# Decay factors of a gated linear attention: one difference for four heads on VectorE and one exponential on ScalarE, in place of four exponentials with a bias

## What is computed

```python
def step(S, inputs):
    qb, kb, vb, lb = inputs
    o_inter = einsum('bhid,bhde->bhie', qb * exp(lb)[..., None], S)
    A = einsum('bhid,bhjd->bhij', qb, kb)
    diff = where(mask, lb[..., :, None] - lb[..., None, :], -inf)
    A = A * exp(diff)
    o_intra = einsum('bhij,bhjd->bhid', A, vb)
    tot = lb[..., -1]
    kd = kb * exp(tot[..., None, None] - lb[..., None])
    S_new = exp(tot)[..., None, None] * S + einsum('bhjd,bhje->bhde', kd, vb)
    return (S_new, o_inter + o_intra)
```

## Time and profile before

| | |
|---|---|
| Median of three runs | 999.23 us (998.97 to 1001.07) |
| Profiled execution | 1001.8 us, its span 1000.1 us |
| TensorE busy | 849.0 us, 85% of the span |
| VectorE busy | 591.0 us, 59% |
| ScalarE busy | 489.6 us, 49% |
| GpSimd busy | 360.4 us, 36% |
| Mean granted TensorE clock | 0.921 of full speed |

### The profile page before, as it was taken

How to read it: one execution, slowest core, us unless ns; L and a number is a source line. 1 busy time by engine, 2 the same in 40 slices (tenths; PEclk the granted TensorE clock), 3 DMA queues, 4 the chain that set the end, 5 groups by cost and what they waited for, 6 DMA issues and landing times.

```text
span 1000.1 us, 15849 instructions
## 1 busy us (share of the span) xinstructions
PE 849.0 (85%) x5650; PEld 686.4 (69%) x5650; DVE 591.0 (59%) x1100; ACT 489.6 (49%) x1131; POOL 360.4 (36%) x277
## 2 busy tenths in 40 slices
PE   1654422999999999999999999999999999999940
PEld 1322211778888888888888887888888888888830
DVE  6652882465566556555656566556655665665584
ACT  2241122654565456546654665566555654554421
POOL 3000013603562446144714371447144714470211
PEclk9965555799999999999999999999999999999975
DMA  7654765646675766576757675766576757662926
GB/s 253 248 213 151 280 162 106 164 153 192 149 173 167 196 154 162 172 195 151 162 178 190 152 158 183 186 161 151 181 189 159 162 172 216 152 149 71 293 74 204
DMA packets 127516, 174.60 MB, mean 175 GB/s; under 512 B 11600, under 2 KB 94544, under 8 KB 125264
## 3 DMA queue, kind: packets, MB, share of 16 engines
q1 hardware_dynamic: 114576, 155.75, 52.8%
q0 software_dynamic: 12288, 16.79, 10.6%
q10 hardware_dynamic: 576, 1.08, 0.3%
HBM read 122.72 MB, written 50.86 MB: 174 GB/s over the span
## 4 chain that ended last, share of the span: by engine, by line
PE 73%; DVE 7%; DMA 4%; ACT 3%; issue 2%; POOL 1%; SPq 0%; ACTq 0%; DVEq 0%; POOLq 0%
PE up_ps L1212 17%; PE y_ps L1238 17%; PE g_ps L1212 16%; PE a_ps L1180 5%; PE m_ps L1134 5%; PE o_ps L1202 5%; PE m_ps L1161 2%; PE m_ps L1142 2%; DMA qk_dram<-qk_r 2%; PE m_ps L1164 1%; PE m_ps L1156 1%; PE o_ps L1195 1%; PE m_ps L1150 1%; ACT dec_both L864 1%; DMA xg<-xn_dram,idx_all 1%
## 5 line engine op out<-in xcount | busy, mean ns | idle before, releaser
L864 ACT ACTIVATE dec_both<-lb_row,neg_lb 128x128 f32<-128x128 f32 x512 | 163.7, 393 | 143.5 <-PE o_ps L1202 139.8
L1238 PE MATMUL y_ps<-w_r,hid_r 128*128 128x256 f32 x1536 | 206.1, 284 | 4.9 <-DVE hid_r L1097 4.9
L1212 PE MATMUL g_ps<-xgt,w_r 128*128 128x512 f32 x768 | 203.3, 400 | 3.1 <-DVE sg L1083 2.5
L1212 PE MATMUL up_ps<-xgt,w_r 128*128 128x512 f32 x768 | 203.6, 401 | 0.0
L1238 PEld LDWEIGHTS y_ps<-w_r,hid_r 128*128 128x128 f32 x1536 | 194.4, 192 | 5.8 <-DVE hid_r L1097 5.1
L770 POOL TENSOR_TENSOR w_r<-w_raw,w_r 128x768 fp32r<-128x768 f32 x64 | 122.1, 1907 | 159.2 <-ACT w_r L884 159.0
L1083 DVE SCALAR_TENSOR_TENSOR sg<-sg,g_ps 128x512 f32<-128x512 f32 x128 | 87.7, 685 | 144.0 <-ACT sg L898 143.9
L1212 PEld LDWEIGHTS up_ps<-xgt,w_r 128*128 128x128 f32 x768 | 139.0, 189 | 26.0
L1212 PEld LDWEIGHTS g_ps<-xgt,w_r 128*128 128x128 f32 x768 | 137.0, 190 | 26.8 <-DVE sg L1083 2.9
L793 POOL DMA_INDIRECT ffn_dram<-y_sb,idx_all x64 | 102.3, 1598 | 142.4 <-DVE y_sb L1032 126.6
L765 POOL TENSOR_SCALAR_AFFINE_SELECT lb_row<-lb_row 128x1024 f32<-128x1024 f32 x64 | 78.0, 1219 | 181.6 <-DMA lb_row<-lb_tiles 181.5
(11 more groups left out here) (167 smaller groups left out, 829.3 us busy)
## 6 DMA issues: line engine op xcount, KB each, us to landing
lb_row<-lb_tiles SPq DMA_DIRECT2D x64, 512.0 KB, 4.3
w_raw<-w_experts SPq DMA_DIRECT2D x64, 384.0 KB, 4.2
qk_dram<-qk_r SPq DMA_DIRECT2D x32, 512.0 KB, 4.3
k_st<-qk_dram SPq DMA_DIRECT2D x96, 128.0 KB, 3.6
arena<-qk_dram SPq DMA_DIRECT2D x192, 64.0 KB, 3.8
xt_dram<-xt SPq DMA_DIRECT2D x8, 1024.0 KB, 4.9
arena<-xt_dram SPq DMA_DIRECT2D x8, 1024.0 KB, 6.9
x_all<-x SPq DMA_DIRECT2D x8, 512.0 KB, 10.0
```

Of the source, the lines that this page charges most:

```text
L864: ins = act.activation(dec[p][:, j, :], lb_row[t // 2 % 2][:, h % HH, :], ACT.Exp, bias=neg_lb[:, ch, h:h + 1])
L1212: mm = pe.matmul(bank[:, :], w_r[:, m, a, at:at + P], xgt[:, b, k, half * 512:(half + 1) * 512], start=(j == 0 and k == 0), stop=(j == len ...
L1238: mm = pe.matmul(y_ps[:, j, :], hid_r[p][:, a, j * P:(j + 1) * P], w_r[:, m, b, DOWN:DOWN + D], start=(m == 0 and q == 0 and j % 2 == 0), ...
```

## The change

The subtraction moves out of ScalarE's bias. VectorE gets a new function `difference`, which adds the masked sums of four heads and the negated sums, one column for each head repeated over 128 columns, and writes `dec`; it takes over the waits for the masked row and for the free buffer. `decays` waits for it (`d_made`) and takes one exponential of 512 columns in place. `difference(0)` stands first on VectorE in `mixed`, `difference(u + 1)` in step u behind `score(u)`. The row buffer is reloaded after the difference.

```diff
 def load_lb(n):
     if n >= 2:
-        sp.wait_ge(e_done, 2 * n - 2)
+        sp.wait_ge(d_made, 2 * n - 2)
...
 def decays(t):
-    ch, g, p = t // NG, t % NG, t % 2
-    act.wait_ge(masked, t // 2 + 1)
-    if t >= 2:
-        act.wait_ge(av_done, t - 1)
-    for j in range(G4):
-        h = g * G4 + j
-        ins = act.activation(dec[p][:, j, :], lb_row[t // 2 % 2][:, h % HH, :], ACT.Exp,
-                             bias=neg_lb[:, ch, h:h + 1])
-    ins.then_inc(e_done, 1)
+    p = t % 2
+    act.wait_ge(d_made, t + 1)
+    act.activation(dec[p], dec[p], ACT.Exp).then_inc(e_done, 1)
...
+def difference(t):
+    ch, g, p = t // NG, t % NG, t % 2
+    dve.wait_ge(masked, t // 2 + 1)
+    if t >= 2:
+        dve.wait_ge(av_done, t - 1)
+    first = g * G4 % HH
+    dve.tensor_tensor(dec[p], lb_row[t // 2 % 2][:, first:first + G4, :],
+                      spread(neg_lb[:, ch, g * G4:(g + 1) * G4], P), ALU.add).then_inc(d_made, 1)
...
     done = 0
+    difference(0)
     for job in FIRST:
         evacuate(job)
...
         if u < TS:
             score(u)
+        if u + 1 < TS:
+            difference(u + 1)
         if first:
             split(first)
```

More of the change, by code:

```diff
@@ L596, in mixed @@
         st_in, qk_out, qk_th, qk_hi, lo_done = pair("st_in"), pair("qk_out"), sem("qk_th"), sem("qk_hi"), sem("lo_done")
+        d_made = sem("d_made")
         e_done, a_done, a_read, av_done = sem("e_done"), sem("a_done"), sem("a_read"), sem("av_done")
```

## The result

The changed kernel takes 1065.12 us (median of 4 runs, 1064.47 to 1067.03), the kernel before 999.35 us beside it. The ratio is 1.0648 with a 95% interval of 1.0629 to 1.0667: 65.8 us slower, where the forecast was 18.2 us and the range ended at 1027.

What follows compares the result with a forecast made beforehand. The prediction took TensorE to bound the long middle; start +5.0 and steps 9 to 11 +13.2 gave +18.2 us, 1020.0 from the profiled 1001.8, forecast as 1017.5 for the median; its range, reaching to A and towards B, was 1003 to 1027.

Steps and rivals of the forecast that it cites:

- The bound: Middle, 300 to 500 us: TensorE busy 199.45 of 200 us, so freeing 83 us of ScalarE is worth nothing by itself.
- the chain that was forecast: Each step: score, then difference, then exponential, 1.84 us from the score's start until ScalarE's next operation starts.
- The price of the difference: VectorE, engine time: one 512-column addition taken as 0.69 us, lower end 0.60, upper end 0.83.
- Steps 9 to 11: Seven of eight batches: later ScalarE results delay TensorE by 0.24, 0.64 and 1.00 us, +13.2 us in all.
- Step 11's q product: The q product at 502.12, priced under step 10: right behind the k result, it slides with it, +0.64 us.
- The start: Before the first gate matmul: +3.1 us to the first gather and input transposes, +1.9 in steps 5 and 6, +5.0 in all.
- The split that had 4.05 us of idle time: Start, VectorE's split at 119.75: its idle time absorbs the 2.8 us slide from difference(0), cost 0.
- Plain steps: ScalarE's next operation slides about 1.0 us, but the hidden half is read 2.9 us after its end: cost 0.
- A: Rival: the middle absorbs the change and only the start pays, 1004 us; chance 0.10.
- B: Rival: lag of 0.2 us builds up in each of 8 weight-copy steps, carried to steps 9 to 11, 1029 us; chance 0.12.
- C: Rival: ScalarE's relief arrives where it was late, in seven batches and the start's chain, 995.7 us; chance 0.03.
- D: Rival: nothing moves, the shifts vanish in slack misread everywhere, 999 us; chance 0.05.

Runs made afterwards that it cites:

- x12: Changed kernel with the difference's second operand in PSUM, differences two steps ahead in three buffers, masks a step earlier, step 9's low half before the scatters: 1002.03 us.
- x1: Changed kernel with only the difference's second operand moved to PSUM, leaving one SBUF input, plus waits protecting that bank: 1026.93 us.
- x2: Kernel before plus an unread 512-column VectorE addition behind each score product, both inputs in SBUF: 1010.62 us.
- x3: Kernel before plus an unread 512-column VectorE addition behind each score product, second input in PSUM, which also signals the scores read: 1002.33 us.
- x6: Changed kernel with the next step's difference ahead of the score product and its second operand in PSUM: 1005.12 us.
- x5: Changed kernel with only the next step's difference put ahead of the score product, still two SBUF inputs: 1024.39 us.

## Why the prediction was wrong

**The bound, and the direction: right.** TensorE sets the middle, relief of ScalarE was worth nothing (x12: none of 83 us), and the change was slower. The direction was no luck: without the stretched differences it is still 2.7% slower (x1), by the chain that was forecast, and TensorE is then busy for 195.77 of the 200 us from 300 on, forecast 195; in the changed kernel it is 187.34.

**The price of the difference: wrong, and this is the failed step.** It is the second paragraph of the part on engine time: I took 0.69 us, from a subtraction with two SBUF inputs, "because column count and memories match", with 0.60 and 0.83 as ends. The row was good for its place: nothing of GpSimd's stood beside it. The new instruction stands elsewhere, 0.6 us behind each score product, and there GpSimd's low half or mask holds it up in 39 of 128 steps. Both were in the trace of before, in the same step 10; I compared sizes and memories and never laid the two timelines side by side. GpSimd's timeline of the kernel before in that step has:

```profile
498.13 2.45 POOL L770 TENSOR_TENSOR w_r<-w_raw,w_r 128x768 fp32r<-128x768 f32 x1
499.95 1.68 POOL L765 TENSOR_SCALAR_AFFINE_SELECT lb_row<-lb_row 128x1024 f32<-128x1024 f32 x1
```

The score product starts at 498.12, so the difference was to start at 498.72, 0.6 us into this pair, which ends at 501.63. VectorE's own two-input products of that step lie outside it, the state product at 497.18 and the split of k at 502.76, and so the trace showed no contention there. What the two rows do give, for an instruction that has to wait for both, is an estimate of 501.63 + 0.69 - 498.72 = 3.6 us in place of my 0.83; in the changed kernel the pair comes 0.8 us later against the score product, and it is 4.27. With one SBUF input the price is 0.68 in all 128 (x1), with two it goes up to 4.27, and x2 against x3 shows this without the rest of the change.

The trace of before has one place with contention, in the top-k search: a copy of 8 columns that takes 0.16 us elsewhere takes 0.67 at 146.94 and ends 0.03 us behind GpSimd's low half (145.78 + 1.80). It has a single SBUF input. In the changed kernel a cast of the same size takes 1.79 us (VectorE, then GpSimd):

```profile
152.61 1.79 DVE L943 CAST top_idx<-i 64x8 f32<-64x8 uint32 x1
```
```profile
152.58 1.80 POOL L771 TENSOR_TENSOR w_r<-w_raw,w_r 128x768 fp32r<-128x768 f32 x1 [6.62 <-ACT w_r L879]
```

So a second SBUF input is not the only way to be held up. x1 has this cast at 1.79 us too, and the same start (first gate matmul at 189.62 and 189.73), so what was told above of the 39 differences is not touched by it.

The Trainium skill states the rule I left out. "SBUF — State Buffer", section "Who interferes with whom": "A DVE instruction with two SBUF inputs contends with a GpSimd instruction that reads SBUF", since both use a shared read interface, and the one that comes second is blocked for the other's whole instruction. The traces agree: 39 of 39 stretched differences end 0.54 to 0.57 us behind such an instruction, and none of x1's 128 is stretched. Which of two comes second can't be read from the starts in the record: the difference at 527.53 starts 0.23 us ahead of the low half that holds it up. The section also says that `tensor_tensor` does not hold up the issuing of descriptors; here 16 of the 17 gathers that run beside a difference of normal length take 0.94 to 1.02 us, and the shortest of the others 0.94.

**Steps 9 to 11: right in size where the difference is not held up.** x1 is the change as I had priced it, and there the chain from the start of the score to the next ScalarE operation is 513.38 - 511.53 = 1.85 us, forecast 1.84. Per batch I had +0.24, +0.64 and +1.00. These terms fall into the intervals of steps 10, 11 and 12, where x1 has +0.5 to +0.8, +0.45 and +1.0, and another +0.3 in step 13, which I had at 0; seven batches 17.7 us against 13.2. The term of step 9 and the missing one of step 13 were too small, that of step 10 a little too large; x1, at 1026.9, lies at the very end of the range.

**Step 11's q product.** Forecast: it slides with the k result, +0.64. Measured: 4.2 us late, because k's tanh stood behind the difference, the exponential, the hidden half and the `e_row` exponential in ScalarE's queue. I had priced the queue and not the case that its head is long. TensorE's half clock behind the 4 us wait then added 1.4 to 2.5 us.

**The start: right, and 0.7 us too small.** Forecast +5.0; the first gate matmul is 6.6 us later, of which 0.9 arose before `mixed` (first k matmul 95.65 against 94.76; over all the traces it lies between 94.3 and 95.8). The indices were to be 1.8 us late; counted from the first k matmul they are 2.6, with the held cast of 1.79 us among them, which the forecast did not have. In the changed kernel difference(0) starts at 101.72 and `k_f` at 102.33. The split that had 4.05 us of idle time has 0.55 and starts at 120.21 instead of 119.75: absorbed, as forecast.

**Plain steps: right.** Over the middle batches the steps other than 5 and 9 to 13 have the same length before and after to within 0.03 us; step 5 has 6.6 to 6.8 instead of 6.49.

**The rivals.** A (the middle absorbs, 1004) fell: the middle pays most. B (a lag that builds up over weight copies) fell: those steps kept their length. C (faster) and D (nothing) fell by the result. The true outcome was none of the four: a contention between two engines that the prediction never considered, though GpSimd's pair stood in the trace at the place where the new instruction was to go.

**How much is what**, by differences of medians: the port with what follows from it 1065.1 - 1026.9 = 38 us; the place of the difference behind the score 22 us (x1 to x6); difference in the chain at all, and the start, 6 us (x6; by the two traces 3.9, of which the start is 1.5). The 22 and the 6 are the forecast's mechanism, the 38 is what it lacked.

## What to carry to other kernels

Before an instruction of two SBUF operands is added to VectorE, lay its place in the step beside GpSimd's timeline: its price is its own duration, or the rest of GpSimd's instruction (here up to two of them) and its own behind that. One operand in PSUM took the price away here, for two small copies in the whole run. A small copy with one SBUF input was held up all the same, so look at those too.

Take an instruction's price from a row in the same surroundings, not from one of the same shape. And look at what an engine's queue holds behind the new instruction: 3.6 us on VectorE became 5.4 to 6.6 us in TensorE's step, since ScalarE's four operations and then the clock stood behind it. Relief of an engine that waited 143 us for others was worth nothing; it cost nothing either only once the new operation had left the chain of its step, two steps ahead in a buffer of its own.

## What the runs showed of the hardware that I had not expected

- The blocked VectorE instruction ends as if all of it ran after GpSimd's: with 512 columns it ends 0.54 to 0.57 us behind it, with 256 columns 0.27 to 0.29 (state update), with 8 columns 0.02. Each is its own duration (0.68, 0.42 and 0.16 us) less some 0.14, though by the record it had started up to 4.2 us before (x5).
- It is held over two GpSimd instructions in a row (low half and mask, 3.5 us together) even though it was waiting ahead of the second: the difference at 527.53 in the changed kernel, the addition at 501.33 in x2.
- GpSimd's low half has 2.4 us in this place instead of 1.84 in the kernel before too, where nothing contends. The record overlaps with the scatter's before it by 0.56 us, so its start may be drawn too early; that was not tried.
- Why x5's difference of step 10 takes 4.7 us in three batches and 0.68 in three others, with the low half 0.68 to 0.71 us behind its start in all six, was not settled.
- After an idle stretch of 4.1 us TensorE's granted clock was 0.50 for the next 4 us and 0.68 over the 4 us after it. Of the six such stretches three were followed by more time at half clock (6.8 us) than the other three (3.4 us); why was not looked into. In the kernel before, whose longest waits of this kind have 0.2 us, the same products ran at 1.00 throughout.
